# Phase one of a two-layer block with a mixture of experts: each engine's order written out operation by operation

## Time and profile before

| what | us |
|---|---|
| median of three executions | 520.96 (520.26 to 523.76) |
| the profiled execution | 516.61 |
| its span | 514.4 |
| PE, DVE, ACT, POOL busy in the span | 406.0, 385.2, 327.3, 259.1 |

### The profile page before, as it was taken

The page is one execution under the profiler, slowest core; times in us unless marked ns, Lnnn a source line. Parts: engine busy times, 40 slices in busy tenths (PEclk is TensorE's granted clock), DMA queues, the critical chain, the costliest instruction groups (busy, mean ns, idle before and its releaser), DMA issues.

```text
span 514.4 us, 13082 instructions
## 1 busy us (share of the span) xinstructions
PE 406.0 (79%) x4092; PEld 306.8 (60%) x4092; DVE 385.2 (75%) x1399; ACT 327.3 (64%) x667; POOL 259.1 (50%) x305
## 2 busy tenths in 40 slices
PE   1447699999999999999999976775988879879810
PEld 0335466766676666666677654554766669667700
DVE  1686689999889888998898782379545367559981
ACT  2344568888788788878888854773545456547610
POOL 3424242454565465647554543347455546457881
PEclk9997799999999999999999988997999999989975
DMA  8462543464466466646755437323544535669974
GB/s 248 133 164 83 163 139 112 144 199 140 154 209 205 125 191 202 186 157 184 216 164 168 150 119 200 88 82 124 148 127 130 154 105 168 218 206 337 331 228 173
DMA packets 74443, 87.09 MB, mean 169 GB/s; under 512 B 9437, under 2 KB 65226, under 8 KB 74250
## 3 DMA queue, kind: packets, MB, share of 16 engines
q1 hardware_dynamic: 66666, 67.39, 44.8%
q0 software_dynamic: 6816, 18.65, 9.7%
q10 hardware_dynamic: 896, 0.23, 0.2%
HBM read 51.07 MB, written 35.18 MB: 168 GB/s over the span
## 4 chain that ended last, share of the span: by engine, by line
DVE 29%; PE 27%; issue 15%; ACT 11%; POOL 9%; another core or an unknown queue 4%; DMA 3%; ACTq 1%; POOLq 0%; SPq 0%; DVEq 0%
PE ps_J L1005 9%; POOL store_y L681 5%; PE ps_T L1015 4%; DVE lg L1461 3%; PE ps_S L1107 3%; ACT xn_B L763 3%; DVE stats_C L1378 2%; PE ps_F L1005 2%; DVE xs L1527 2%; PE ps_R L1182 2%; PE ps_R L1047 2%; ACT xn_C L763 2%; POOL result L675 2%; DVE stats_B L1378 2%
## 5 line engine op out<-in xcount | busy, mean ns | idle before, releaser
L681 POOL DMA_INDIRECT store_y<-y_out,y_row x78 | 78.8, 1011 | 57.9 <-DVE y_out L1903 40.6
L668 POOL DMA_INDIRECT store_x<-xn_E,slot_u x64 | 64.2, 1002 | 26.6 <-issue 16.6
L819 ACT ACTIVATE prob<-ps_S 128x512 f32<-128x512 f32 x128 | 72.1, 594 | 0.5 <-PE ps_S L1107 0.3
L1891 DVE TENSOR_TENSOR h_lo<-h_f,h_hi 128x512 f16<-128x512 f32 x39 | 29.1, 747 | 40.5 <-ACT h_hi L888 38.0
L1107 PE MATMUL ps_S<-q_stack,k_stack 128*128 128x256 f16 x256 | 44.0, 276 | 8.2 <-ACT prob L819 7.9
L1120 PE MATMUL ps_O<-prob,v_wide 128*32 128x128 f32 x1024 | 41.2, 279 | 0.3 <-ACT prob L819 0.3
L641 POOL TENSOR_TENSOR rstd_B<-var_B,minus_half 128x2 f32<-128x2 f32 x16 | 11.7, 734 | 56.8 <-DVE var_B L1387 56.8
L1005 PE MATMUL ps_J<-wout_hi,h_hi 128*128 x112 | 31.2, 278 | 11.0 <-DVE y_out L1903 8.8
L646 POOL TENSOR_TENSOR inv_norm<-norm2c,minus_half 128x2 f32<-128x2 f32 x16 | 11.0, 690 | 53.5 <-DVE norm2c L1453 53.5
L1107 PEld LDWEIGHTS ps_S<-q_stack,k_stack 128*128 128x128 f16 x256 | 20.4, 98 | 27.8 <-ACT prob L819 16.8
L1434 DVE TENSOR_TENSOR parts<-ps_J,parts 128x512 f16<-128x512 f32 x32 | 22.1, 691 | 19.0 <-ACT parts L814 18.7
(11 more groups left out here) (284 smaller groups left out, 1439.5 us busy)
## 6 DMA issues: line engine op xcount, KB each, us to landing
xb<-store_x SPq DMA_DIRECT2D x39, 257.0 KB
parts_scratch<-parts SPq DMA_DIRECT2D x32, 256.0 KB, 2.1
k_stack<-parts_scratch SPq DMA_DIRECT2D x64, 128.0 KB
q_stack<-parts_scratch SPq DMA_DIRECT2D x128, 64.0 KB, 2.3
y_got<-store_y SPq DMA_DIRECT2D x16, 512.0 KB
x_in<-in_x SPq DMA_DIRECT2D x16, 256.0 KB
c_in<-in_ctx SPq DMA_DIRECT2D x16, 256.0 KB
out<-result SPq DMA_DIRECT2D x16, 256.0 KB
```

Of the source, the lines that this page charges most:

```text
L668: pool.indirect_dma_start(store_x, bass.IndirectOffsetOnAxis(slot_u[q][:, at:at + 1], 0), xn_e[q][:, at, :], None).then_inc(s_scat[q], 16)
L681: pool.indirect_dma_start(store_y, bass.IndirectOffsetOnAxis(y_row[n][:, b:b + 1], 0), y_out[n][:, b, :], None).then_inc(s_y_kept[n], 16)
L819: act.activation(prob[m % PROBS][:, 2 * n:2 * n + 2, :, :], bank_s[n], ACT.Sigmoid, scale=float(HD) ** -0.5).then_inc(s_prob[n], 1)
L1891: dve.tensor_tensor(h_lo[q][:, :, :], h_f32[q][:, :, :], h_hi[q][:, :, :], ALU.subtract) .then_inc(s_h_lo, 1)
```

## The change

Nothing that is computed changes, and no buffer. The loops over t and the helpers `live` and `prior` are gone; phase one is a list of calls on each engine, with an order of its own for each body. The use of a bank that came before is now an argument, as in `keys(("v", 9), 10)`. `base_product` and `values` have a wait of their own for the halves that they read. Set-up steps are functions, called where the list has them. In the start the layer norms A of pairs 0 and 1 come first, `scan(0)`, `scan(1)` and `scan(2)` come ahead of the first product, the identity is the first DMA of ScalarE instead of the fifth, and SyncE loads two expert matrices and the context of pair 2 ahead of the constants. Blocks 0 to 14 are written out too, with the final plan's 25 steps spread over them, and seven of the last eight scatters stand among the output scatters of blocks 0 to 9. Each engine's start, one body from the middle and the passage to phase two, from the diff (a line "..." is a cut):

SyncE:

```diff
     load_ctx(0)
+    load_weights(s_wkv, C_K, C_Q)
     load_x(1)
+    load_weights(s_wrest, C_Q, WCOLS)
+    load_weights(s_wbase, C_BASE, C_K)
     load_ctx(1)
+    load_ups()
+    load_matrix(0)
+    load_ctx(2)
+    load_matrix(1)
+    load_x(2)
+    load_constants()
+    load_x(3)
+    load_ctx(3)
+    load_matrix(2)
+    load_projection()
+    sp.wait_ge(s_zero, 4)
+    zero_first(0)
+    keep_parts("k", 0)
+    keep_parts("k", 1)
+    load_ctx(4)
+    load_x(4)
+    keep_parts("q", 0)
+    stack_keys(0)
+    zero_first(1)
+    stack_queries(0)
+    zero_first(2)
+    zero_first(3)
+    zero_first(4)
+    zero_first(5)
+    zero_first(6)
+    zero_first(7)
+    load_x(5)
+    stack_keys(1)
+    keep_parts("q", 1)
...
+    load_x(11)
+    load_ctx(11)
+    stack_keys(8)
+    keep_parts("k", 9)
+    keep_parts("q", 8)
+    load_x(12)
+    stack_queries(8)
+    load_ctx(12)
...
+    zero_spare(6)
+    load_biases()
+    load_block(0)
+    load_block(1)
     keep_parts("q", 15)
+    load_block(2)
+    load_block(3)
     stack_queries(15)
+
+    for i in range(4, TILES):
```

GpSimd:

```diff
+    small_constants()
+    blank_queries(0)
+    inverse_root("A", 0)
+    squared(0)
+    inverse_root("A", 1)
+    squared(1)
+    make_x1(0)
+    similarity_roots()
+    inverse_root("B", 0)
+    squared(2)
+    blank_values(0)
+    blank_queries(1)
+    make_x1(1)
+    inverse_norm(0)
...
+    scatter(4, 1)
+    make_x1(9)
+    inverse_norm(8)
+    scatter(4, 0)
+    scatter(4, 2)
+    inverse_root("B", 9)
+    squared(10)
+    inverse_root("C", 8)
...
+    inverse_root("E", 15)
+    scatter(14, 3)
     keep_block(0, 0)
     keep_block(0, 1)
+    scatter(14, 0)
     keep_block(1, 0)
     keep_block(1, 1)
+    scatter(15, 3)
+    keep_block(2, 0)
+    keep_block(2, 1)
+    keep_block(3, 0)
+    keep_block(3, 1)
+    scatter(14, 1)
+    keep_block(4, 0)
+    keep_block(4, 1)
+    keep_block(5, 0)
+    keep_block(5, 1)
+    scatter(14, 2)
+    scatter(15, 2)
+    scatter(15, 1)
+    keep_block(6, 0)
+    keep_block(6, 1)
+    keep_block(7, 0)
+    keep_block(7, 1)
+    keep_block(8, 0)
+    keep_block(8, 1)
+    keep_block(9, 0)
+    keep_block(9, 1)
+    scatter(15, 0)
```

ScalarE:

```diff
+    gates_tanh()
+    gained(0)
     weights_hi(s_wkv, C_K, C_Q - C_K)
+    gained(1)
+    matrix_hi(0)
+    hi_ctx(0)
+    temperature_exp()
+    weights_hi(s_wbase, C_BASE, C_K - C_BASE)
+    matrix_hi(1)
+    normed_b(0)
+    small_weights_hi()
+    hi_b(0)
+    identity_half()
+    ups_hi()
+    part_hi("k", 0)
+    gate_sigmoids(0)
+    spread_values(0)
+    hi_ctx(1)
+    copy_down(0)
+    weights_hi(s_wrest, C_Q, C_SMALL - C_Q)
+    gained(2)
+    normed_b(1)
...
+    copy_av(14)
+    copy_hi(1)
+    output_rows(13)
+    sigmoids(15, 0, 0)
     sigmoids(15, 0, 1)
+    normed_e(14)
+    sigmoids(15, 1, 0)
     sigmoids(15, 1, 1)
+    sigmoids(15, 2, 0)
     sigmoids(15, 2, 1)
+    sigmoids(15, 3, 0)
     sigmoids(15, 3, 1)
     hi_e(14)
     copy_av(15)
     gelu(0)
     hidden_hi(0)
+    output_rows(14)
+    output_rows(15)
     copy_hi(2)
     gelu(1)
     hidden_hi(1)
     normed_e(15)
     copy_hi(3)
     gelu(2)
     hidden_hi(2)
+    hi_e(15)
+    copy_hi(4)
+    gelu(3)
+    hidden_hi(3)
     gate_ratios()
```

TensorE:

```diff
+    pe.wait_ge(s_ident, 16)
+    transpose_ctx(None, 0)
     pe.wait_ge(s_decay, 16)
+    scan(0)
+    similarity_sums()
+    scan(1)
+    similarity_products()
+    transpose_b(("T", 0), 0)
+    scan(2)
+    pe.wait_ge(s_wlo, 3)
+    small_product(None, 0)
+    pe.wait_ge(s_wlo, 1)
+    keys(None, 0)
+    transpose_ctx(("B", 0), 1)
+    pe.wait_ge(s_wlo, 2)
+    base_product(0)
+    pe.wait_ge(s_wlo, 1)
+    values(("k", 0), 0)
+    transpose_down(("small", 0), 0)
+    add_ups(0)
+    keys(("v", 0), 1)
+    scan(3)
+    transpose_c(("T", 1), 0)
+    transpose_b(("C", 0), 1)
+    pe.wait_ge(s_wlo, 4)
+    queries(("k", 1), 0)
+    small_product(("down", 0), 1)
+    transpose_ctx(("B", 1), 2)
+    base_product(1)
+    values(("q", 0), 1)
+    transpose_down(("small", 1), 1)
+    add_ups(1)
...
+    keys(("v", 9), 10)
+    scores(8, 0, 0)
+    transpose_c(("T", 10), 9)
+    scores(8, 0, 1)
+    scan(11)
+    scores(8, 1, 1)
+    transpose_b(("C", 9), 10)
+    queries(("k", 10), 9)
+    weigh(8, 0)
+    scores(8, 1, 0)
+    small_product(("rank", 6), 10)
+    base_product(10)
+    transpose_e(("B", 10), 7)
+    scores(8, 2, 1)
+    values(("q", 9), 10)
+    scores(8, 2, 0)
+    scores(8, 3, 1)
+    weigh(8, 1)
+    logits(("small", 10), 7)
+    scores(8, 3, 0)
+    weigh(8, 2)
+    transpose_down(("logits", 7), 10)
+    weigh(8, 3)
+    add_ups(10)
+    transpose_ctx(("E", 7), 11)
+    project(8)
+    ranks(("down", 10), 7)
...
     transpose_block(0)
+    weigh(14, 3)
+    logits(("rank", 12), 13)
+    project(14)
+    transpose_block(1)
+    layer1(0, 0)
+    layer1(0, 1)
+    ranks(("logits", 13), 13)
+    scores(15, 0, 0)
     scores(15, 0, 1)
+    scores(15, 1, 0)
     scores(15, 1, 1)
+    transpose_block(2)
     weigh(15, 0)
+    transpose_e(("E", 13), 14)
+    scores(15, 2, 0)
     scores(15, 2, 1)
     weigh(15, 1)
+    scores(15, 3, 0)
     scores(15, 3, 1)
     weigh(15, 2)
     weigh(15, 3)
+    logits(("rank", 13), 14)
     project(15)
+    ranks(("logits", 14), 14)
     layer1(1, 0)
     layer1(1, 1)
     layer2(0, 0)
     layer2(0, 1)
```

VectorE:

```diff
+    blank_tiles()
+    statistics_a(0)
+    means("A", 0)
+    variances("A", 0)
+    statistics_a(1)
+    means("A", 1)
+    gain(0)
+    shifts_a(0)
+    variances("A", 1)
+    clamp_temperature()
+    moves(0)
+    gain(1)
+    square_similarities()
+    shifts_a(1)
+    weights_lo(1, C_K, C_Q - C_K)
+    similarities()
+    statistics_b(0)
+    means("B", 0)
+    variances("B", 0)
+    scaled_similarities()
+    lo("T", 0, ct_hi[:, :, :], ct_lo[:, :, :])
+    shifts("B", 0)
+    moves(1)
+    small_weights()
+    weights_lo(2, C_BASE, C_K - C_BASE)
+    weights_lo(3, C_SMALL, WCOLS - C_SMALL)
+    statistics_a(2)
+    lo("B", 0, xt_hi["B"][:, :, :], xt_lo["B"][:, :, :])
+    constants()
+    means("A", 2)
+    copy_small(0)
+    squares(0)
+    clamp_norm(0)
+    statistics_b(1)
+    adapter_logits(0)
+    variances("A", 2)
+    adapter_max(0)
+    adapter_diff(0)
+    part_lo("k", 0)
+    adapter_code(0)
+    adapter_ratio(0)
+    adapter_win(0)
+    adapter_exp(0)
+    gain(2)
+    means("B", 1)
+    adapter_picked(0)
+    adapter_sum(0)
+    variances("B", 1)
+    adapter_down(0)
+    adapter_top(0)
+    adapter_gated(0)
+    shifts_a(2)
+    down_hi(0)
+    down_lo(0)
+    statistics_a(3)
+    means("A", 3)
+    lo("T", 1, ct_hi[:, :, :], ct_lo[:, :, :])
+    make_x2(0)
+    statistics_c(0)
+    shifts("B", 1)
+    means("C", 0)
+    variances("C", 0)
+    moves(2)
+    shifts("C", 0)
+    weights_lo(4, C_Q, C_SMALL - C_Q)
+    variances("A", 3)
+    matrix_lo(0)
...
+    moves(11)
+    lo("B", 10, xt_hi["B"][:, :, :], xt_lo["B"][:, :, :])
+    shifts("E", 7)
+    part_lo("q", 9)
+    copy_small(10)
+    squares(10)
+    clamp_norm(10)
+    statistics_b(11)
+    variances("A", 12)
+    means("B", 11)
+    adapter_logits(10)
+    adapter_max(10)
+    adapter_diff(10)
+    lo("E", 7, xt_hi["E"][:, :, :], xt_lo["E"][:, :, :])
+    adapter_code(10)
+    adapter_ratio(10)
+    adapter_win(10)
+    adapter_exp(10)
+    adapter_picked(10)
+    adapter_sum(10)
+    adapter_down(10)
+    adapter_top(10)
+    variances("B", 11)
+    adapter_gated(10)
+    down_hi(10)
+    copy_logits(7)
+    down_lo(10)
+    router_max(7)
+    statistics_a(13)
+    router_index(7)
+    router_picks(7)
+    router_diff(7)
+    shifts("B", 11)
+    make_x2(10)
+    router_both(7)
+    statistics_c(10)
+    means("C", 10)
+    variances("C", 10)
+    lo("T", 11, ct_hi[:, :, :], ct_lo[:, :, :])
+    shifts("C", 10)
...
     router_picks(15)
+    router_diff(15)
+    take_rows(4)
     router_both(15)
+    hidden_lo(3)
+    add_bias(2)
     rank_rows(15)
     rank_picked(15)
     slots(15)
+    next(final)
+    next(final)
+    copy_lo(5)
+    take_rows(5)
+    next(final)
+    next(final)
+    next(final)
+    hidden_lo(4)
+    add_bias(3)
+    copy_lo(6)
     next(final)
     next(final)
     next(final)
     next(final)
     next(final)
+    take_rows(6)
+    hidden_lo(5)
+    add_bias(4)
     next(final)
     next(final)
     next(final)
     next(final)
+    copy_lo(7)
+    take_rows(7)
+    hidden_lo(6)
+    add_bias(5)
+    copy_lo(8)
+    next(final)
+    take_rows(8)
+    hidden_lo(7)
+    add_bias(6)
+    next(final)
+    copy_lo(9)
     next(final)
     next(final)
+    take_rows(9)
+    hidden_lo(8)
+    add_bias(7)
+    copy_lo(10)
     next(final)
     next(final)
+    take_rows(10)
+    hidden_lo(9)
+    add_bias(8)
+    next(final)
+    copy_lo(11)
+    take_rows(11)
+    hidden_lo(10)
+    add_bias(9)
+    copy_lo(12)
     next(final)
     next(final)
+    take_rows(12)
+    hidden_lo(11)
+    add_bias(10)
     next(final)
+    copy_lo(13)
+    take_rows(13)
+    hidden_lo(12)
+    add_bias(11)
+    copy_lo(14)
     next(final)
```

(5 more changed lines are left out.)

2257 lines of the change are left out of this document (1775 added, 482 removed).

## The result

The changed kernel takes 515.32 us (median of nine executions, 511.37 to 525.58), before 520.72 in the same series; the ratio is 0.9896, with an interval of 0.9853 to 0.9939. So it is 1% faster, 5 us, where I had forecast 18 us and a range that ends at 515.0. Direction right, size wrong. A ratio uses only the executions within 1.5% of the fastest of their kernel, a median uses all.

The account below looks back on a forecast made before the run. Waiting was taken as the bound: dependent steps at the start, TensorE 94% busy in the middle. Gains 5.5 + 2.4 + 5.2 + 2 + 3 = 18.1 us took 516.61 to 498.5; with 4.35 for the median, 503.0, range 492 to 515.

Parts of the forecast that it names:

- The start: Start to x2 of pair 0: reordered chain brings x2 from 37.03 to 31.3 us; 5.5 us gain taken, ends 0 and 7.4.
- the sign that I had named: In the start: x2 of pair 0 near 31.5 us, with VectorE waiting for the constants just before.
- Bodies 1 and 2: The two bodies after x2 of pair 0: 16.8 instead of 18.0 us each, together 2.4 us gained.
- The 13 bodies: x2 of pair 2 to pair 15: waits shrink 0.4 us a body, 5.2 in all; ends 2.6 lost, 12.7 gained.
- two edits: In each body: base product ahead of third scores (0.58 us wait); GpSimd's x1 and squares moved (adapter chain 1 us shorter).
- the lags between pairs are the same: In the 13 bodies: lags between pairs stay as before; only the order inside a body differs.
- rival 4: GpSimd's squares, x1 and scatters hit VectorE steps between `copy_small` and `make_x2`: 22 us lost, 532 us; chance 0.07.
- Passage: Passage to phase two: block 0's transposition and first layer fill attention waits; 2 us gain, ends 4 lost and 6 gained.
- Blocks: Blocks 1 to 5 and final plan: spreading gains 4 us, late plan costs 1; together 3, ends 3 lost and 8.6 gained.
- rival 1: Only the ends gain: 10.9 us from start, bodies 1 and 2 and plan, the rest 0; 510 us, chance 0.20.
- 3: Rival of no change: late constants and pair 1 loads; last query rows give back the plan's gain; 519 to 521, chance 0.10.
- rival 5: A DMA or semaphore holds one engine's list and all others once, some 5 us: 508 us, chance 0.08.

Follow-up runs that it names:

- again: The changed kernel once more, nothing edited, on a fast chip: 482.16 us, 0.9915 of before.
- g_start: Changed order up to x2 of pair 2, everything behind as before, cut by work already done; slower chip: 510.15 us, 0.9895 of before.
- g_mid: Changed kernel with each engine's order from x2 of pair 2 to x2 of pair 14 as before; slower chip: 516.54 us, 1.0015 of before.
- a_zeros: Changed kernel with four of six first writes of zeros in one SyncE row moved later; slower chip: 513.36 us, 0.9949 of before.
- g_zeros: g_start with four of six first writes of zeros in one SyncE row moved later; slower chip: 507.03 us, 0.9905 of before.
- before_look: The kernel before once more, nothing edited, for its trace on a slower chip; before took 515.23 us there.
- g_zeros2: g_zeros once more, nothing edited, on a slower chip: 505.76 us, 0.9983 of before.
- g_plan: g_zeros with VectorE's 25 final plan steps spread over blocks 4 to 14 as in the change; slower chip: 508.18 us, 0.9979 of before.
- e_base: Kernel before with the base product ahead of the third pair of score products in each body: 513.76 us, one execution.
- e_squares: Kernel before with GpSimd's squares of the next pair behind root B instead of ahead of x1: 518.48 us, one execution.
- start_only: Changed order of the start (to the keys of pair 2), all else as before, cut by pair numbers; fast chip: 482.96 us, 0.9947 of before.
- e_split: Kernel before with two of each body's four scatters moved behind the root of layer norm E on GpSimd: 532.96 us, one execution.
- mid_regular: Changed kernel with the bodies of pairs 3 to 14 in the order of before, cut by pair numbers; fast chip: 483.92 us, 0.9973 of before.
- a_single: Changed kernel, zeros spread, scatters of pairs 0 to 9 moved so none stands directly behind another; fast chip: 487.98 us, 1.0058 of before.
- g_best: g_mid with zeros spread and layer norm C's root of pair 14 ahead of pair 10's four scatters; slower chip: 513.12 us, 0.9954 of before.
- b_single: Kernel before with each body's four GpSimd scatters placed singly behind root A, root E, squares and x1; fast chip: 592.18 us, 1.2179 of before.

## Why the prediction was wrong, step by step

**The start: right in size, in part by luck.** The copy of the small product is at 23.54 (22.9 forecast) and x2 of pair 0 at 30.94 (31.3). In all traces x2 of pair 0 lies between 30.9 and 32.5 with the new start and between 35.6 and 37.4 with the old one. But two errors cancelled on the way. I had `constants` wait for its last DMA until 22.3. That DMA, issued at 17.95, landed 2.3 us later, not 4.9, and VectorE did not wait for it: the sign that I had named did not come. `constants` began at 22.24 because the lower half of B was done only at 22.32, where I had 21.6. B's normalised tile was late by 1.3 us, since the shift, forecast at 17.4, ended at 18.67: beside GpSimd's squares of pair 2 it took 0.99 us.

**Bodies 1 and 2: right in size,** 3.1 us against 2.4 in this execution. In the later ones it is 0.4 to 3.6 us, x2 of pair 2 lies between 63.4 and 68.0, which I had not allowed for, and in again, g_start and g_mid the next body takes 18.9 to 19.8 us; the scores wait up to 2.2 us there, by my reading for query rows.

**The 13 bodies: the step that failed.** I had put it as "I take 0.4, 13 × 0.4 = 5.2 us; the ends are a loss of 0.2 a body (2.6) and the floor, 12.7". Measured: 11.0 us lost in the first execution, 6.3 in a_zeros (215.1 us from pair 3 to 15, against 208.8 in g_zeros on the same chip), 4.3 on the fast chip. The regular order took 208.6 to 208.8 us there in all six traces with it on the slower chips, before, before_look, g_start, g_zeros, g_zeros2 and g_plan. So the loss is the order's, but for 3.4 us at pair 12 (21.85 against 18.45) that a_zeros does not have. My own sign of being wrong, bodies above 17.3 us, came: 18.2 in the mean. How the loss divides between the causes below is not measured. Three errors lie in it.
- I priced two edits of a list that had hundreds, and took the gain of each as what the wait in the earlier trace rows showed. e_base and e_squares, each edit alone, gain nothing: the first moves its wait to three others, the second makes the body 0.2 us longer. lg did fall to 0.17 us in every body of the change, as forecast, and that freed 9.0 us of VectorE's time in the 13 bodies. The shifts of B, C and E and the step `picks` took 11.5 us more, and VectorE was busy 205.2 us against 203.4. Each shift above 0.3 us ran beside squares or x1. By the rule of the Trainium skill's "SBUF — State Buffer" ("Who interferes with whom"), which I had weighed against this edit, the collision is only moved; these steps agree, and e_squares too, with lg 0.70 us beside x1.
- I took "the lags between pairs are the same" to mean that the loss is bounded by 0.2 us a body. The order within a body is as tight: on the fast chip TensorE waits in the changed kernel 5.6 us for lower halves of the context and 2.8 for xn_C, between 100 and 290, and in start_only, with the regular order, neither is among its waits.
- I looked at GpSimd's scatters only as neighbours of small VectorE steps (rival 4). On the slower chips what falls beside a row of them is held, and where it lies decides. Before, what fell there was the copy of the query halves, 0.94 us in each body. The irregular order has it at a different place each time, 1.6 us at pair 5, 3.4 and 0.9 at pair 6. Rival 4 named the collisions with VectorE's small steps, and they came, at the shifts; it did not have the held results.

The shift of E in the 13 bodies of before and of the change, on VectorE (ns: shortest, median, longest):

```profile
L1393 DVE SCALAR_TENSOR_TENSOR shift_E<-mv_E,rstd_E x13: 148/150/154, 83.1 to 292.0; 128x2 f32<-128x2 f32 x13
L2363 DVE SCALAR_TENSOR_TENSOR shift_E<-mv_E,rstd_E x13: 149/493/823, 71.7 to 289.8; 128x2 f32<-128x2 f32 x13
```

**Passage: the number met, the gain not shown.** It gave 1.8 us against 2 in the first pair of traces. From x2 of pair 15 to the output of block 0 the later traces of slower chips have 40.6 to 42.0 us with the new passage and 39.7 to 41.7 with the old one (e_split left out), and on the fast chips 38.2 to 38.8 (again, mid_regular, a_single) against 37.8 in start_only. The 1.8 was luck. **Blocks: the sum is off.** Blocks 1 to 5 gave 4.8, and the later ones took 4.1 back where I had charged 1. And the plan is not what gave it: alone, in g_plan, it makes blocks 1 to 5 longer by 2.6 us. The whole tail to block 38 takes 166.9 to 167.3 us on the fast chips against 169.6 in start_only, 2.5 us of the 5 that I had summed; on the slower ones the two overlap (190.0 to 195.4 against 188.7 to 193.6). The waits of the earlier trace rows that I meant to fill stand behind ScalarE's waits for the first layer, some of which are put down to "remote" too (9.6 us in 4 waits from 339 to 414 before). That these are why the filling gave nothing is argued, not shown.

**Rivals and range.** What came is nearest to rival 1 (ends gain, bodies not), with a loss in the bodies where it had none. I had given it 0.20 and 510. I had bounded the loss in the bodies by 2.6; with that and the other terms as taken the sum is 510.7, and 515 was too low for the 11.0 that came. The rivals that the range leaves out are 3 and 4; the prediction says "the last two", but rival 5 lies inside it.

**Open:** why TensorE's results reach the others late beside a row of scatters, and only on some chips; no trace of before itself was taken on a fast chip. Single scatters that are early enough were not tried on a slower chip. What stops the last body of g_mid and g_best. Removing the scatters from phase one was not tried, since the rows that phase two loads would then be undefined. No kernel here is shown to beat the change: g_start (0.9895) is level with it, and g_zeros and g_zeros2, 8 us below before by their medians, have wide intervals, 0.9826 to 0.9983 and 0.9906 to 1.0059.

## What to carry to other kernels

A steady loop whose bound engine is 94% busy has its waits where its order puts them; take one away and measure the body, not the wait, since here the next one was already there. Walk a start-up chain step by step, and check the steps and not only the sum; don't add up local gains in a loop. Look at a gain in several executions before you call its mechanism right. Before an order is changed, look up which transfers have a latest time of issue and what stands beside a row of GpSimd's DMAs.

## What the runs showed of the hardware

- The same kernel takes 485 us on some chips and 514 to 521 on others, at a granted clock of 0.94 to 0.96 in both and with equal durations. In the regular bodies the difference is about one wait of 0.94 us beside the row of scatters, 17.5 against 16.64 us. Two thirds of the 30 us lie in phase two: blocks 1 to 38 in the same order take 151.5 us in g_start and 131.9 in start_only.
- Late release beside a row of GpSimd's indirect DMAs, 3.4 us behind the end of the product in one case and 2.0 in another. 174 waits in thirteen traces of slower chips are put down to "remote", and 100 of them end 0.4 to 1.1 us behind the last scatter in front; the seven traces of fast chips have none.
- From the issue of a scatter of 128 rows to the release of its tile 2.9 to 4.0 us pass (11 bodies of b_single), while its record takes 1.0.
- Small VectorE steps with two SBUF inputs grow when their place moves beside GpSimd's: the shift of E from 0.15 to 0.49 us in the median, while lg fell from 1.00 to 0.17.
